# A decoder layer on one core: full-row bias passes for the grouped experts, warming matmuls, routing in five groups, and weight loads behind the context

## The reference

```
logits = x @ Wr.T + br;  top_v, top_i = top_k(logits, 2);  top_w = softmax(top_v)
h = relu(x @ W1[e].T + b1[e])            # 512 wide
o = h @ W2[e].T + b2[e]                  # 128 wide
x = layernorm(x + sum over the two of top_w * o) * gamma + beta
```

## Time and profile before

| | us |
|---|---|
| median of 3 runs (308.35 to 313.68) | 308.64 |
| the profiled execution | 308.13 |
| its span, first to last instruction | 306.2 |
| TensorE busy in the span | 229.2 |
| VectorE | 151.4 |
| ScalarE | 100.0 |
| GpSimd | 64.6 |

### The profile page before, as it was taken

The page is one execution under the profiler, slowest core; times in us unless marked ns, Lnnn a source line. Parts: engine busy times, 40 slices in busy tenths (PEclk is TensorE's granted clock), DMA queues, the critical chain, the costliest instruction groups (busy, mean ns, idle before and its releaser), DMA issues.

```text
span 306.2 us, 4604 instructions
## 1 busy us (share of the span) xinstructions
PE 229.2 (75%) x1518; PEld 144.5 (47%) x1518; DVE 151.4 (49%) x407; ACT 100.0 (33%) x194; POOL 64.6 (21%) x73
## 2 busy tenths in 40 slices
PE   5999497698898398298683604999999999997000
PEld 4456243354466166165662602666656666665000
DVE  5586999946656356247776600222212212220493
ACT  1469771424345235234322000212222221222043
POOL 9100000000006401101117880121222122123200
PEclk9999689999999699689956755555555555555555
DMA  6999944003736995976501112221000000000301
GB/s 176 250 242 217 399 191 139 0 1 99 185 93 207 312 261 192 302 200 218 168 14 47 40 38 45 70 69 31 17 18 9 19 14 7 19 0 2 120 16 45
DMA packets 13560, 34.40 MB, mean 112 GB/s; under 512 B 2141, under 2 KB 5790, under 8 KB 13538
## 3 DMA queue, kind: packets, MB, share of 16 engines
q1 hardware_dynamic: 12354, 32.25, 36.3%
q0 software_dynamic: 1184, 1.86, 2.0%
HBM read 27.99 MB, written 6.56 MB: 113 GB/s over the span
## 4 chain that ended last, share of the span: by engine, by line
PE 47%; DVE 26%; DMA 10%; ACT 7%; issue 5%; POOL 3%; SPq 2%; ACTq 0%; DVEq 0%; POOLq 0%
PE bank L654 12%; PE bank L666 9%; PE bank L651 6%; DMA ctxT_slot<-ctx_T 5%; DVE sums L1040 5%; PE bank L494 5%; PE bank L429 4%; PE bank L509 2%; POOL slots L1448 2%; DVE sums L1076 2%; DMA xpad<-x_T 2%; PE bank L450 1%; PE bank L641 1%; PE bank L500 1%; PE bank L662 1%
## 5 line engine op out<-in xcount | busy, mean ns | idle before, releaser
L1346 DVE SCALAR_TENSOR_TENSOR ctx_slot<-bank,ctx_slot 128x512 f16<-128x512 f32 x21 | 14.5, 692 | 62.2 <-ACT ctx_slot L885 62.2
L1474 POOL DMA_INDIRECT ret<-ctx_slot,ctxT_slot x21 | 20.5, 974 | 79.0 <-ACT ctx_slot L892 78.3
L885 ACT ACTIVATE ctx_slot<-bank 128x512 f16<-128x512 f32 x21 | 12.5, 597 | 72.0 <-PE bank L654 72.0
L494 PE MATMUL bank<-ctxT_slot,qk_sb 97*64 97x500 f32 (+1 forms) x96 | 25.7, 678 | 11.9 <-DMA ctxT_slot<-ctx_T 10.9
L654 PE MATMUL bank<-ctx_slot,terms 128*128 128x128 f16 x168 | 33.2, 302 | 0.0
L1432 POOL CAST rows<-rows_late 112x256 f16<-112x256 f32 x8 | 5.5, 689 | 121.1 <-DVE rows_late L1275 121.1
L654 PE MATMUL bank<-ctx_slot,sums 128*128 128x128 f16 x84 | 26.4, 314 | 0.0
L666 PE MATMUL bank<-terms,ctx_slot 128*128 x168 | 26.1, 311 | 0.0
L651 PE MATMUL bank<-w_conv 40*128 x84 | 24.0, 286 | 0.6 <-DVE ctx_slot L1339 0.6
L429 PE MATMUL bank<-xpad,w_conv 128*128 128x448 f32 x48 | 21.3, 608 | 1.9 <-DMA xpad<-x_T 1.9
L1152 DVE TENSOR_REDUCE neg_max<-bank 120x1 f32<-120x1500 f32 x8 | 13.7, 1717 | 16.2 <-PE bank L494 16.2
(11 more groups left out here) (188 smaller groups left out, 410.4 us busy)
## 6 DMA issues: line engine op xcount, KB each, us to landing
ctx_slot<-ctx SPq DMA_DIRECT2D x16, 576.0 KB, 8.0
ctxT_slot<-ctx_T SPq DMA_DIRECT2D x16, 562.5 KB, 7.7
w_raw<-w SPq DMA_DIRECT2D x16, 256.0 KB, 3.2
slots<-w_raw SPq DMA_DIRECT2D x4, 910.0 KB, 27.0
ctxT_slot<-slots SPq DMA_DIRECT2D x21, 65.0 KB, 1.8
ctxT_slot<-ret SPq DMA_DIRECT2D x4, 224.0 KB, 3.5
convw_sb<-conv_w SPq DMA_DIRECT2D x3, 256.0 KB, 6.3
small_sb<-small SPq DMA_DIRECT2D x1, 611.5 KB, 10.1
```

The costliest lines, as they stand in the source:

```text
L494: mm = pe.matmul(bank[j * GAP:j * GAP + rows, n, 0:SN], qk_sb[:, j * L:j * L + rows], ctxT_slot[:, s, j, n * SN:(n + 1) * SN], start=True, ...
L1346: V.scalar_tensor_tensor(hl[:, t % 3].rearrange("p f t -> p (f t)"), bank[:, t % 3, :], 0.0, hh[:, t % 3].rearrange("p f t -> p (f t)"), A ...
L1474: G.indirect_dma_start(ret[:], bass.IndirectOffsetOnAxis(ap=xs_u[:, t, D + 1:D + 2], axis=0), out_st[:, t % OB, :], None, bounds_check=2 * ...
```

## The change

- `BK` is 128 instead of 40. `b1_hl`, `b2_hl`, `pick`, `b2_ones` and the bias load take all 128 partitions; the added rows are zeros in the bias array and in the `eye` that `pick` is made of. The number of passes is unchanged.
- `GROUPS` has five groups: pairs 0 and 1, 2 and 3, 4 and 5, 6, 7. `choose` is cut in two (`top_two` and `choose`). The choice of group 0 moves to the end of VectorE's turn 4, that of group 1 to the end of turn 6; their `ranks` are in TensorE's turns 5 and 7, `place` and `route_weights` in VectorE's turns 5 and 7. The last split of weights moves behind the tile map. GpSimd scatters group 0 behind the rows of pair 4, groups 1 and 2 behind those of pair 6, groups 3 and 4 behind those of pair 7.
- SP loads the weights of expert i + 1 in turn i (from i = 1 on), when expert i - 1 is split, and the last behind the loop.
- `keep_warm` stands in more places: 1, 4 and 2 matmuls between the last steps of the routing, 12 instead of 6 at its end, 10 behind the last tile.
- The returned rows are summed on TensorE: x2, and the two rows of each token, are multiplied with the identity and accumulated in PSUM; VectorE reads the sums there. GpSimd's two adds are gone, and `summed` applies gamma before it waits for the root.

```diff
-BK = 40
-GROUPS = (range(0, 4), range(4, 6), range(6, 7), range(7, 8))
+BK = 128
+GROUPS = (range(0, 2), range(2, 4), range(4, 6), range(6, 7), range(7, 8))
...
                 sp_.wait_ge(a_pv, i + 1)
                 ctx_rows(i + 2, s)
-                sp_.wait_ge(m_wl, 2 * i + 2)
-                load_w(0, i + 2, s)
-                load_w(1, i + 2, s)
+                if i:
+                    sp_.wait_ge(m_wl, 2 * i)
+                    load_w(0, i + 1, 1 - s)
+                    load_w(1, i + 1, 1 - s)
+            sp_.wait_ge(m_wl, 2 * (PAIRS - 2))
+            load_w(0, PAIRS - 1, 1)
+            load_w(1, PAIRS - 1, 1)
...
-                if last:
-                    ranks(0)
+                if i in (5, 7):
+                    ranks((i - 5) // 2)
...
             turn_x2(PAIRS - 2)
-            ranks(1)
+            ranks(2)
             pe.wait_ge(a_x2T, PAIRS)
             turn_sum(PAIRS - 1)
             logits(PAIRS - 2)
+            keep_warm(1, 5)
             values(PAIRS - 1)
-            ranks(2)
+            keep_warm(4, 5)
             turn_x2(PAIRS - 1)
+            ranks(3)
             logits(PAIRS - 1)
-            ranks(3)
+            keep_warm(2, 5)
+            ranks(4)
             totals()
-            keep_warm(6, 6)
+            keep_warm(12, 5)
...
+            def summed(q, rows_, start=False, stop=False):
+                return pe.matmul(bank[0:PT, q, 0:2 * D], ident[0:PT, 0:PT], rows_, start=start, stop=stop)
+
+            pe.wait_ge(t_hl, TILES)
+            for q in range(4):
+                summed(q, x2[:, 2 * q:2 * q + 2, :], start=True)
+            keep_warm(10, 7)
+            for q in range(4):
+                pe.wait_ge(g_ld[q], 16)
+                summed(q, got[:, 2 * q:2 * q + 2, 0, :])
+                summed(q, got[:, 2 * q:2 * q + 2, 1, :], stop=True).then_inc(f_y, 1)
...
# VectorE, turn i
                     attended(i - 1)
+                    if i in (5, 7):
+                        place((i - 5) // 2)
                     split_low(0, i - 1)
                     attended_norm(i - 1)
                     split_low(1, i - 1)
-                if last:
-                    place(0)
-                    route_weights(0)
-                if i + 1 == PAIRS - 1:
-                    choose(0)
+                if i in (5, 7):
+                    route_weights((i - 5) // 2)
+                if i in (4, 6):
+                    top_two((i - 4) // 2)
+                    choose((i - 4) // 2)
...
# VectorE, last norm
+            def returned(q):
+
+                dve.wait_ge(f_y, q + 1)
+                for j in (0, 1):
+                    a = own.mark(V.bn_stats(stat[:, 2 * q + j, :], bank[0:PT, q, j * D:(j + 1) * D]))
                 own.need(a)
...
# GpSimd
-                if i >= 5:
-                    scatter(i - 5)
+                if i == 4:
+                    scatter(0)
+                if i == 6:
+                    scatter(1)
+                    scatter(2)
             scatter(3)
+            scatter(4)
```

More of the change, by code:

```diff
@@ L234, in decoder_kernel @@
         turn16 = [bank[:, n, :].bitcast(F16) for n in (3, 7)]
[L237 to L239 removed]
+        logit_at = [bank[0:PT, n, 256:256 + E] for n in (6, 6, 6, 6, 6, 2, 2, 2)]
+        rank_at = [bank[0:PT, n, 320:320 + len(g) * E].rearrange("p (i e) -> p i e", e=E)
+                   for n, g in zip((6, 1, 0, 1, 0), GROUPS)]
+        total_at = bank[0:32, 4, 0:E]
         nmr = sb("nmr", [PT, PAIRS])
@@ L536, in ranks, with before @@
                 a, b = pairs[0], pairs[-1] + 1
-                def at(j):
-                    return rank_at[n][:, j - a:, :]
+                def before(j, start=False, stop=False):
+                    to = max(a, j + 1)
+                    return pe.matmul(rank_at[n][:, to - a:, :], ones16[0:PT, 0:PT],
+                                     sel[:, j, :].unsqueeze(1).broadcast_to([PT, b - to, E]), start=start, stop=stop)
                 if n == 0:
                     pe.wait_ge(s_consts, 1)
-                if n >= 2:
+                if n >= 3:
                     pe.wait_ge(r_rk, n - 1)
+                for j in range(a):
+                    before(j, start=(j == 0))
                 pe.wait_ge(r_sel, n + 1)
[L546 to L550, removed]
+                mm = pe.matmul(rank_at[n], before16[:], sel[:, a:b, :], start=(a == 0), stop=(b == a + 1))
+                for j in range(a, b - 1):
+                    mm = before(j, stop=(j == b - 2))
                 mm.then_inc(r_rank, 1)
@@ L1177, in choose @@
                 V.tensor_tensor(tsm[:, 0, w], top[:, w, 1], top[:, w, 0], ALU.subtract).then_inc(r_diff, 1)
+            def choose(n):
+                pairs = GROUPS[n]
+                a, b = pairs[0], pairs[-1] + 1
+                w = slice(a, b)
                 dve.wait_ge(r_idx, b)
@@ L1313, in _ @@
             logit_read(PAIRS - 3)
-            choose(1)
+            top_two(2)
+            choose(2)
             sum_copy(PAIRS - 1, 1)
             x2T_copy(PAIRS - 2)
-            place(1)
-            route_weights(1)
+            place(2)
+            route_weights(2)
             attended(PAIRS - 1)
             logit_read(PAIRS - 2)
+            top_two(3)
             attended_norm(PAIRS - 1)
-            choose(2)
+            choose(3)
             x2T_copy(PAIRS - 1)
[L1324 to L1328, removed]
             place(3)
             route_weights(3)
+            logit_read(PAIRS - 1)
+            top_two(4)
+            choose(4)
+            route_weights(4)
+            place(4)
             tile_map()
+            split_low(0, PAIRS - 1)
             split_low(1, PAIRS - 1)
@@ L1357, in _ @@
                     hidden_low(t + 1)
-            def stats(tiles, done):
-                for j in tiles:
-                    a = own.mark(V.bn_stats(stat[:, j, :], acc[:, j, :]))
+            def returned(q):
+                dve.wait_ge(f_y, q + 1)
+                for j in (0, 1):
+                    a = own.mark(V.bn_stats(stat[:, 2 * q + j, :], bank[0:PT, q, j * D:(j + 1) * D]))
                 own.need(a)
[L1364 to L1379, removed]
+                for j in (0, 1):
+                    a = V.bn_aggr(mv[:, 2 * q + j, :], stat[:, 2 * q + j, :])
+                a.then_inc(f_var, 1)
             def summed(q):
                 dve.wait_ge(m_x2b, 1)
+                dve.wait_ge(f_var, q + 1)
+                for j in (2 * q, 2 * q + 1):
+                    a = own.mark(V.scalar_tensor_tensor(acc[:, j, :], bank[0:PT, q, (j % 2) * D:(j % 2 + 1) * D],
+                                                        mv[:, j, 0:1], par("gamma", PT), ALU.subtract, ALU.mult))
+                own.need(a)
                 dve.wait_ge(f_rstd, q + 1)
[L1385 to L1388, removed]
                 for j in (2 * q, 2 * q + 1):
@@ L1392, in summed @@
                 own.need(a)
-                stats((2 * q, 2 * q + 1), f_var2)
+                for j in (2 * q, 2 * q + 1):
+                    a = own.mark(V.bn_stats(stat[:, j, :], acc[:, j, :]))
+                own.need(a)
+                dve.wait_ge(f_rstd, q + 1)
+                for j in (2 * q, 2 * q + 1):
+                    a = V.bn_aggr(mv[:, j, :], stat[:, j, :])
+                a.then_inc(f_var2, 1)
             def final_bias(q):
@@ L1476, in _ @@
                                      ).then_inc(t_sc[t % OB], 16)
[L1478 to L1481, removed]
     return nc
```

34 lines of the change are left out of this document (19 added, 15 removed).

## The result

The changed kernel takes 266.83 us (median of 4 runs, 265.73 to 267.74) where the kernel before took 310.82 beside it: a ratio of 0.863, 95% interval 0.858 to 0.869. The forecast was 264, with a range of 250 to 280. The profiled execution is 266.64 us with a span of 264.9. Some executions of one kernel here are 1 to 2% slower than its others, and ratios are taken from the fast ones alone.

What follows compares the result with a forecast made beforehand. TensorE's chain was taken to bound the experts, GpSimd's scatters the stretch before them, late context the attention. Experts -26.6, context -9.0, scatter -7.4 and end -1.0 sum to -44.0, giving 264 us, range 250 to 280.

Steps and rivals of the forecast that it cites:

- The experts: Expert tiles: full-row bias passes and a risen clock bring a tile from 4.44 to 3.15 us, -26.6 us in all.
- rival 3: Experts: the 40 rows aren't what costs, step and low clock stay, 291 us; chance 0.08.
- Rival 1: Experts: register instructions overlap with the array's work, a tile takes 1.66 to 2.3 us, total 233 to 247; chance 0.07.
- The context: Attention: with weight loads issued behind the context, scores wait less: -9.0 us, bounds -4 and -13.
- from there DMA is the bound: Attention from pair 4's scores on: DMA sets the turns at 10.0 us each, pair 7's scores at 127.0.
- some 2 us in several turns: Attention, sign of being right: scores wait some 2 us for context in several turns and never 5.
- The 1.5 counted: Attention: 1.5 us for two added routing blocks on VectorE, 1.3 us each, partly hidden by waits for DMA.
- Rival 2: Attention: the context gains nothing because DMA was busy anyway, 274 us; chance 0.07.
- rival 4: Attention: late expert weights delay ScalarE's split, exponentials and context in a loop, 18.2 us a turn, 318 us; chance 0.02.
- The scatter: Routing: 12 GpSimd issues left behind the last turn, the last at 173.7 instead of 181.07, -7.4 us.
- nothing waits for them: Before the experts: tile map and last weight splits are done by 174, tiles start at 181, so no cost.
- +0.8: Last norm: VectorE reads the sums from PSUM in 16 instructions at 0.05 us more each, +0.8 us.

Runs made afterwards that it cites:

- e1: The changed kernel with BK back at 40, all else kept: 293.5 us, 0.945 of the kernel before.
- e2: The kernel before with BK at 128 and nothing else of the change: 285.4 us, ratio 0.917.
- e3: The changed kernel with each tile's expert number fixed in the program instead of loaded, so tiles go through the wrong expert: 239.4 us, ratio 0.769.
- e8: The changed kernel with the expert numbers of the first 11 tiles loaded into registers before the first tile: 260.4 us, ratio 0.830.
- e4: The changed kernel with SP's old order of weight loads (expert i + 2 in turn i): 277.7 us, ratio 0.891.
- e9: One of the twelve follow-up kernels; the text doesn't tell which change or measured time belongs to this label.
- e7: The changed kernel with BK at 64: 275.7 us (one run).

## Why the prediction was right, point by point

**The experts** carried it. The chain's 0.22 us for a 40-row pass was put down to the rows, by comparing L651 with L662 and L666; 40, 64, 100 and 128 rows bear it out, and rival 3 fell with e1 and e2. The Trainium skill's rule in "TensorE: Matmul & The Clock Gate", section "LDWEIGHTS (loading the stationary operand)", that a weight load's time goes by its columns and not its rows, agrees with the load taken alone: in the kernel before, a 40-row load takes 102 ns and the 128-row load right behind it 105. What the 40 rows cost is not in the load's length but in where it stands, behind the pass before it instead of under it.

**The clock** rose 3.5 us into the stage, as forecast, and as forecast it was worth little. The sum over the sequencer's records, 3.1 us, was taken as 3.15 and came out at 3.22; its bounds of 2.9 and 3.3 held. Rival 1 would have been right for a kernel without registers: e3 has its 1.74 us. The Trainium skill's 81 ns for a weight load and its pass ("TensorE: Matmul & The Clock Gate", section "Back-to-back issue gap") are not what bounds a tile here: without register work a pair takes 56 ns, and the tile is 1.74 us, with it 3.22. The 2.53 us of e8 equal the estimate of 2.5 by chance, for its tiles still carry register work.

**The context** gained 7.5 where 9.0 was written. The step that was off is "from there DMA is the bound": that holds for pair 5 alone (10.9 us from pair 4's scores, 10.0 forecast, with 1.03 DMA share and 327 GB/s in between). The turns behind it take 9.2 and 10.7 us, and there the chain runs through VectorE's splits, choice and maximum, with only 0.61 us of waiting for DMA in front of pair 7's scores. So the sign "some 2 us in several turns" was met in one turn alone. Of the two added blocks only the choice, 1.5 us on the chain, lies ahead of pair 7's scores; places and weights come behind their start, from 129.58 on, and are paid in the next stretch. The 1.5 counted was thus right for this stretch, by luck, as it had been meant for both blocks less a hidden part. Rival 2 fell with e4, and rival 4's wait for weights didn't come up.

**The scatter** gained 5.1 of 7.4; the last one stands 13.5 us earlier, where the sign said 16. One part: GpSimd started at 151.56 with group 1's weights, 22.4 us behind pair 7's scores where 21.2 were expected; places had moved, but the weights still stand behind the splits. The other is one scatter of 2.11 us where the others take 0.94:

```profile
162.70 2.11 POOL L1481 DMA_INDIRECT slots<-rows,slot_i  x1 [0.15 <-POOL rows L1469]
```

It starts with the last two splits of weights on VectorE, which the change had put side by side:

```profile
162.70 1.27 DVE L1102 SCALAR_TENSOR_TENSOR sums<-w_raw,terms 128x512 f16<-128x512 f32 x2
```

The forecast put the moved splits at nothing ("nothing waits for them"); it looked at who waits for their result, not at what runs beside them. No run takes the splits away, but the traces settle it by when a scatter happens to start. In all fourteen no scatter into `slots` takes over 1.13 us unless it starts during a split. Started with the first of two, it takes 2.11 us (five traces); started 0.3 us into it, 1.81 (e3, e4, e9); and one that starts before the pair isn't held, but the next one is, for 0.2 us, as in e1:

```profile
162.66 0.96 POOL L1481 DMA_INDIRECT slots<-rows,slot_i  x1 [0.16 <-POOL rows L1469]
162.99 1.27 DVE L1102 SCALAR_TENSOR_TENSOR sums<-w_raw,terms 128x512 f16<-128x512 f32 x2
163.93 1.15 POOL L1481 DMA_INDIRECT slots<-rows,slot_i  x1 [0.30 <-issue]
```

The held scatters end 0.8 us behind the end of the last split, whenever they started. It cost 1.2 us here and 0.2 in e1, which differs in nothing that bears on it: whether the two meet is luck.

**The end** gained 1.6 and not 1.0: VectorE's first step comes 1.15 us behind the data, from it to the start of its last it is 12.4 us where it was 15.3, and reading PSUM cost nothing: statistics take 281 ns from PSUM and 285 from SBUF. The +0.8 for it is the term that was wrong.

The terms' errors were +0.2 (experts), +1.5 (context), +2.3 and +0.1 (scatter and what follows it) and -0.6 (end), 3.5 us together. That the total was off by 2.6 alone is luck: 0.9 us of the gain lie in the first stage, which nobody touched.

## What to carry to other kernels

A busy engine at a low clock has three bounds in it, array, clock and sequencer, and raising one shows the next: before counting on a doubled clock, add up what the sequencer has to do for each tile from its own records. Passes with few rows are not cheaper than full ones, and with 40 or 64 rows among full ones each cost 0.2 us more here, because weight loads were no longer hidden; zeros in the unused rows cost TensorE nothing. What an instruction costs its neighbours is not seen by asking who waits for its result: look at what runs beside it on engines that stand on the path. A value loaded into a register should carry its bounds, and loads of such values belong into the waits in front of a loop.

## What had not been expected of the hardware

- The clock's rise in e7: tiles alike, with 64-row passes, ran ten at the low clock and the rest at the high one, where 40-row passes in three kernels never rose in 21 tiles. What decided the moment stays open; e7 was run once.
- A change between a narrow and a full pass costs 0.11 us at the low clock and 0.10 at the high one: the weight load there isn't hidden.
- A GpSimd scatter issue of 2.11 us where 0.94 is usual, when it starts with two VectorE splits from fp32 to fp16: it ends some 0.8 us behind them.
- Register instructions of 18 to 60 ns take 0.08 to 0.12 us of the sequencer each, and show nowhere among the busy times of the page.
